# A decoder layer with a recurrent state and 64 routed experts: other loads at the start, states ordered head first, routing one iteration later

## The reference

```python
x = L0_attn_x
xn = _layernorm(x, axis=-1)
x = x + _L0_attn_ref(xn, ...) + _L0_ffn_ref(xn, ...)
```

```python
def step(Sst, inp):
    q_t, k_t, v_t, b_t, g_t = inp
    Sst = Sst * g_t[..., None, None]
    kS = jnp.einsum('bhk,bhkv->bhv', k_t, Sst)
    Sst = Sst + b_t[..., None, None] * jnp.einsum('bhk,bhv->bhkv', k_t, v_t - kS)
    o_t = jnp.einsum('bhk,bhkv->bhv', q_t, Sst)
    return (Sst, o_t)
```

## Time and profile before

| | us |
|---|---|
| median of 3 runs | 2108.34 |
| lowest, highest | 2107.29, 2110.54 |
| the profiled execution | 2116.39 |
| its span, first to last instruction | 2114.7 |
| mean granted TensorE clock, share of full speed | 0.808 |

### The profile page before, as it was taken

One profiled execution on the slowest core, in us unless ns is written; L12 is line 12 of the kernel. 1 busy time (PEld: TensorE's weight loads), 2 busy tenths in 40 slices (PEclk: granted clock), 3 DMA queues, 4 the chain that ended last, 5 costly groups with the idle time before them and its releaser, 6 DMA issues. The chain is left out here.

```text
span 2114.7 us, 32382 instructions
## 1 busy us (share of the span) xinstructions
PE 1507.1 (71%) x8894; PEld 1306.1 (62%) x8894; DVE 1863.5 (88%) x6189; ACT 876.7 (41%) x2296; POOL 1629.1 (77%) x1340
## 2 busy tenths in 40 slices
PE   6477878887751777655656558887888888868538
PEld 5467767776641666555555547776777777757336
DVE  3149999999998899999998798999999999999990
ACT  3355465546530442323423246545554344333113
POOL 4527888788886778877878689888888889888861
PEclk9778878877875877778777669988999899979677
DMA  8634233433336545565454621233222311111111
GB/s 192 154 90 119 60 86 88 131 89 85 87 82 155 140 115 134 138 177 138 104 143 125 169 64 53 61 99 93 64 57 73 106 51 43 54 54 35 38 35 26
DMA packets 302281, 201.30 MB, mean 95 GB/s; under 512 B 176210, under 2 KB 289556, under 8 KB 302100
## 3 DMA queue, kind: packets, MB, share of 16 engines
q1 hardware_dynamic: 283780, 165.40, 28.8%
q0 software_dynamic: 16208, 33.56, 7.2%
q10 hardware_dynamic: 2112, 0.26, 0.1%
HBM read 127.58 MB, written 71.60 MB: 94 GB/s over the span
## 5 line engine op out<-in xcount | busy, mean ns | idle before, releaser
L795 POOL TENSOR_TENSOR rp<-S,qs 128x2048 f32<-128x2048 f32 x113 | 514.0, 4549 | 173.8 <-DVE S L1087 128.9
L1087 DVE SCALAR_TENSOR_TENSOR S<-S,gwin,bank 128x256 f32<-128x256 f32 x1024 | 481.8, 471 | 1.1
L1081 DVE TENSOR_TENSOR bank<-nu,bank 128x256 f32<-128x256 f32 x1024 | 431.6, 421 | 1.1
L1071 DVE TENSOR_REDUCE bank<-prod 128x16 f32<-128x256 f32 x1024 | 429.9, 420 | 1.1
L1066 DVE TENSOR_TENSOR prod<-S,bank 128x256 f32<-128x256 f32 x1024 | 423.7, 414 | 0.5 <-DVE bank L1163 0.3
L1659 PE MATMUL bank<-region 128*128 128x128 f32 x2048 | 286.5, 300 | 0.0
L1659 PEld LDWEIGHTS bank<-region 128*128 128x128 f32 x2048 | 272.8, 214 | 16.3 <-issue 15.9
L803 POOL TENSOR_TENSOR r<-rp 128x1024 f32<-128x1024 f32 x113 | 274.8, 2432 | 7.1
L1670 PE MATMUL bank<-region 128*128 128x256 f32 x1024 | 236.7, 385 | 5.5 <-DVE region L1054 5.5
L1558 PE MATMUL bank<-xaT,wqkvg 128*128 128x128 f32 (+1 forms) x1792 | 236.1, 290 | 3.3 <-ACT xaT L1267 3.0
L1076 DVE SCALAR_TENSOR_TENSOR nu<-bank,gwin,win_v 128x16 f32<-128x16 f32 x1024 | 234.3, 229 | 1.1
(11 more groups left out here) (155 smaller groups left out, 2479.1 us busy)
## 6 DMA issues: line engine op xcount, KB each, us to landing
qkv_d<-stg SPq DMA_DIRECT2D x64, 384.0 KB, 4.1
region<-in_L_ffn_w_gate SPq DMA_DIRECT2D x64, 192.0 KB, 3.4
region<-in_L_ffn_w_up SPq DMA_DIRECT2D x64, 192.0 KB, 3.8
region<-in_L_ffn_w_down SPq DMA_DIRECT2D x64, 192.0 KB, 4.3
win_k<-qkv_d SPq DMA_DIRECT2D x16, 512.0 KB
win_q<-qkv_d SPq DMA_DIRECT2D x16, 512.0 KB
win_v<-qkv_d SPq DMA_DIRECT2D x16, 512.0 KB
region<-in_L_attn_x SPq DMA_DIRECT2D x32, 256.0 KB, 4.4
```

The source lines that it names most:

```text
L795: g.tensor_tensor(rp[:, :, :].rearrange("p (a v) d -> p a v d", v=DH), S[h][:, lo:lo + HS].rearrange("p t s (v d) -> p (t s) v d", v=DH), ...
L1071: m[G] = mark(v.tensor_reduce(kS[:, G], prod[:, G].rearrange("p (v d) -> p v d", v=DH), AX.X, ALU.add))
L1081: m[G] = mark(v.tensor_tensor(outer.rearrange("p (v d) -> p v d", v=DH), nu[:, G].unsqueeze(2).to_broadcast([P, DH, DH]), key(s, G), ALU.m ...
L1087: ins = v.scalar_tensor_tensor(S[h][:, s, G], earlier(h, s, G), gwin[:, I // NB2 & 1, G, 1, t:t + 1], outer, ALU.mult, ALU.subtract)
```

## The change

- SyncE loads blocks 0 to 3 of x and the ln1 weights' matrices first, straight to where they are used; ScalarE's queue loads ln1's gain and bias, which are applied to the transposed tile at its evacuation (two instructions in place of one) and no more to the weights. Constants for routing and the back are loaded behind the 16 stores, and block 4 of x with them. Blocks 5 to 7 are loaded in iterations 2 to 4, and the statistics and factors of blocks 4 to 7 are taken in iterations 1 to 4.
- The factors are worked out from the variance in closed form: one power for the front, one for routing, a block at a time.
- Partitions of states are ordered (head, sequence) where they were (sequence, head); the o stores are two DMAs where they were one.
- Block 0's window is loaded by GpSimd's queue, keys first; a separate semaphore tells of keys. VectorE squares and sums the keys of half 1 and scales block 0's keys.
- Routing iterations are 1 to 16, all later stages one iteration later; iteration 0 has a front tile only. The back's iteration without a tile is gone.
- The queries' copy stands at the end of every iteration. The window's load stands before the iteration's front store.

Cut to its core:

```diff
-R1 = 2 * NB2
+NRT = 2 * NB2
+R0 = 1
+R1 = R0 + NRT
...
-REFILL = {SEG[1]: FILL + 23, SEG[2]: FILL + 27}
+REFILL = {SEG[1]: FILL + 23, SEG[2]: FILL + 26}
...
-    counts = (3, 2, 3, 2, 3, 2, 3, 2, 2, 2, 3, 3, 0, 1, 2, 1)
+    counts = (3, 2, 3, 2, 3, 2, 3, 2, 2, 2, 3, 3, 1, 2, 1)
...
+LATE = 3
 FST = 2 * 16
-WLD = 5 * 16
+WLD = 4 * 16
+KLD = 16
+OST = 2 * 16
...
-        qkv_ld = qkv_d.rearrange("k (s b) (m g) (h d) t -> k m s b (g h) (d t)", s=2, m=3, h=P // DH)
-        gat_ld = gat_d.rearrange("k (s b) w h t -> k s w b h t", s=2)
-        o_st = o_d.rearrange("k (s b) g (h v) t -> k (b g h) s (v t)", s=2, h=P // DH)
+        qkv_ld = qkv_d.rearrange("k (s b) (m g) (h d) t -> k m s (g h) b (d t)", s=2, m=3, h=P // DH)
+        gat_ld = gat_d.rearrange("k (s b) w h t -> k s w h b t", s=2)
+        o_st = o_d.rearrange("k (s b) g (h v) t -> k s (g h) b (v t)", s=2, h=P // DH)
...
+            key_in, rest_in = keys_in(k, s)[0], window_in(k, s)[0]
+            queue.dma_start(win[1][:, par, s].rearrange("p d t -> p (d t)"), qkv_ld[k, 1, s]).then_inc(key_in, 16)
+            queue.dma_start(win[2][:, par, s].rearrange("p d t -> p (d t)"), qkv_ld[k, 2, s]).then_inc(rest_in, 16)
+            for w in range(2):
+                queue.dma_start(gwin[:, par, s, w], gat_ld[k, s, w]).then_inc(rest_in, 16)
+            queue.dma_start(win[0][:, par, s].rearrange("p d t -> p (d t)"), qkv_ld[k, 0, s]).then_inc(rest_in, 16)
...
-
             for m, w in enumerate((Wq, Wk, Wv)):
-                sp.dma_start(wraw[:, :, m * D:(m + 1) * D], w.rearrange("(c p) n -> p c n", p=P)).then_inc(raw_ld, 16)
+                sp.dma_start(wqkvg[:, :, m * D:(m + 1) * D], w.rearrange("(c p) n -> p c n", p=P)).then_inc(raw_ld, 16)
             for m, w in enumerate((Wb, Wg)):
-                sp.dma_start(wraw[:, :, 3 * D + m * H:3 * D + (m + 1) * H],
+                sp.dma_start(wqkvg[:, :, 3 * D + m * H:3 * D + (m + 1) * H],
                              w.rearrange("(c p) n -> p c n", p=P)).then_inc(raw_ld, 16)
-            for m, w in enumerate((ln1_g, ln1_b, ln2_g, ln2_b)):
-                sp.dma_start(lncol[:, m, :], w.rearrange("(c p) -> p c", p=P), allow_slow_non_contiguous=True).then_inc(raw_ld, 16)
+            for k in range(1, 4):
+                load_xs(sp, k)
...
+                done = f_stored[i] if k else first_st[q // (NB2 // 2)][i]
+                sp.dma_start(qkv_st[k, q], stg[i].rearrange("p b i t -> p (b i) t")).then_inc(done, 16)
+                sp.dma_start(gat_st[k, q], gst[i].rearrange("p (b t) -> p b t", b=2)).then_inc(done, 16)
...
-                window_half(k + 1, (k + 1) & 1, (k + 2) * NB2, s)
+                for i in range(BUF):
+                    sp.wait_ge(f_stored[i], (min((k + 1) * NB2 + s, NT - NB2) + 1 - i) // 2 * FST)
+                sp.sem_inc(passed, 1)
+                window_loads(sp, k + 1, (k + 1) & 1, s)
...
+            for f in range(AHEAD * NB2):
+                front_store(f, f // NB2, f % NB2, f % 2)
+                if f == NB2 + 1:
+                    for i in range(2):
+                        sp.sem_inc(xt_ld[i], AHEAD * NB2 // 2 * 16)
+                        front_load(AHEAD * NB2 + i, AHEAD, i, i)
...
+            load_xs(sp, 4)
+            sp.dma_start(wo_s[:, :, :], Wo.rearrange("(c p) n -> p c n", p=P)).then_inc(mlp_in, 16)
+            sp.dma_start(bo_s[:, :], bo.rearrange("(a n) -> a n", a=1)).then_inc(mlp_in, 16)
+            sp.dma_start(b1_in[:, :], b1.rearrange("(c p) -> p c", p=P), allow_slow_non_contiguous=True).then_inc(mlp_in, 16)
+            for m, w in enumerate((ln2_g, ln2_b)):
+                sp.dma_start(lncol[:, 2 + m, :], w.rearrange("(c p) -> p c", p=P), allow_slow_non_contiguous=True).then_inc(mlp_in, 16)
...
+                if 2 <= I < 2 + LATE:
+                    sp.wait_ge(xs_used, I + 3)
+                    load_xs(sp, I + 3)
...
+                    if 0 <= i < NRT - 1:
+                        route_load(i + 1, (i + 1) // NB2, (i + 1) % NB2, (i + 1) % 2)
                     if j < 2:
                         next_window(I // NB2, j)
-                    if I > 1:
-                        weights_store(I - 2)
-                        count_store(I - 2)
+                    front_store(f, f // NB2, f % NB2, h)
...
+            def front_factors(k):
+
+                lo, hi = k * NB2, (k + 1) * NB2
+                pool.wait_ge(xs_used, k + 1)
+                link(g.tensor_scalar(tmp_st[:, lo:hi], var[:, lo:hi], 1.0 + EPS, EPS * EPS, ALU.mult, ALU.add))
+                g.tensor_scalar(nmean[:, lo:hi], mean[:, lo:hi], -1.0, None, ALU.mult)
+                link(power(sA[:, lo:hi], tmp_st[:, lo:hi], 0, hi - lo))
+                g.tensor_tensor(bA[:, lo:hi], nmean[:, lo:hi], sA[:, lo:hi], ALU.mult).then_inc(stats_done, 1)
+
+            def route_factors(k):
+
+                lo, hi = k * NB2, (k + 1) * NB2
+                pool.wait_ge(stats_done, k + 1)
...
+                link(power(rstd[:, lo:hi], tmp_st[:, lo:hi], 0, hi - lo))
+                g.tensor_tensor(nmr[:, lo:hi], nmean[:, lo:hi], rstd[:, lo:hi], ALU.mult).then_inc(rstd_done, 1)
+
+            for k in range(2):
+                front_factors(k)
+            for k in range(2):
+                route_factors(k)
+            for k in range(2, 4):
+                front_factors(k)
+                route_factors(k)
             relink()
+            for s in range(2):
+                for i in range(BUF):
+                    pool.wait_ge(first_st[s][i], NB2 // 4 * FST)
+                pool.sem_inc(passed, 1)
+                window_loads(pool, 0, 0, s)
...
+            scale_values(0, 0)
+            square_sums(0, 0)
+            scale_values(0, 1)
             scale_gates(0)
-            for s in range(2):
-                scale_keys(0, s)
+
...
+                    if 1 <= I <= 1 + LATE:
+                        front_factors(I + 3)
+                        route_factors(I + 3)
...
+                    for s in range(2):
+                        g.dma_start(o_st[I // NB2, s], oblk[:, s].rearrange("p v t -> p (v t)")).then_inc(o_stored, 16)
...
+            def late_stats(k, part, c):
+
+                if part == 0:
+                    dve.wait_ge(xs_ld[4], 32 * (k - 3))
+                    for q in range(NB2):
+                        c[0] = mark(v.bn_stats(bn6[:, q, :], xs[4][:, q, :]))
+                elif part == 1:
+                    dve.wait_ge(vch, c[0])
+                    for q in range(NB2):
+                        c[0] = mark(v.bn_aggr(mv8[:, q, :], bn6[:, q, :]))
+                else:
+                    dve.wait_ge(vch, c[0])
+                    link(v.tensor_copy(mean[:, k * NB2:(k + 1) * NB2], mv8[:, :, 0]))
+                    v.tensor_copy(var[:, k * NB2:(k + 1) * NB2], mv8[:, :, 1]).then_inc(xs_used, 1)
...
+            def first_squares():
+
+                dve.wait_ge(*keys_in(0, 1))
+                dve.wait_ge(n2_ready, 1)
+                link(v.tensor_tensor(sq[:, :], win[1][:, 0, 1].rearrange("p d t -> p (d t)"),
+                                     win[1][:, 0, 1].rearrange("p d t -> p (d t)"), ALU.mult))
+                dve.sem_inc(sq_ready, 1)
+                v.tensor_reduce(n2[:, 1, :], sq[:, :].rearrange("p (d t) -> p t d", t=BLK), AX.X, ALU.add).then_inc(n2_ready, 1)
+
+            def first_keys():
+
+                dve.wait_ge(rk_ready, 1)
+                for s in range(2):
+                    kw = win[1][:, 0, s]
+                    v.tensor_tensor(kw, kw, rk[:, s, :].unsqueeze(1).to_broadcast([P, DH, BLK]), ALU.mult).then_inc(keys_ready, 1)
+
+            first_squares()
...
+                    if r is not None and (R0 <= I < R1 or X0 <= I < X1):
+                        product((I - R0 if I < R1 else I - X0 + NRT) * RT + r, r)
+                    if 1 <= I <= 1 + LATE and s >= 5:
+                        late_stats(I + 3, s - 5, t_)
...
-            act.wait_ge(raw_ld, 16 * 9)
-            for c in range(DC):
-                a_.activation(wqkvg[:, c, :], wraw[:, c, :], ACT.Copy, scale=lncol[:, 0, c:c + 1]).then_inc(w_scaled, 1)
-            act.wait_ge(bias_mm, 1)
-            a_.activation(bqkv[:, 0:2], LG[:, 0:2], ACT.Copy, scale=DH ** -0.5).then_inc(bias_done, 1)
-            a_.activation(bqkv[:, 2:6], LG[:, 2:6], ACT.Copy).then_inc(bias_done, 1)
-            a_.activation(bqkv[0:2 * H, 6:7], LG[0:2 * H, 6:7], ACT.Copy).then_inc(bias_done, 1)
-            act.wait_ge(bias_done, 3)
+            for m, w in enumerate((ln1_g, ln1_b)):
+                a_.dma_start(lncol[:, m, :], w.rearrange("(c p) -> p c", p=P), allow_slow_non_contiguous=True).then_inc(ln_ld, 16)
...
-                a_.activation(xaT[i].rearrange("p c t -> p (c t)"), banks[0][:, 0:DC * P], ACT.Copy).then_inc(xaT_ready, 1)
+                for c in range(DC):
+                    last = a_.activation(xaT[i][:, c, :], banks[0][:, c * P:(c + 1) * P], ACT.Identity,
+                                         scale=lncol[:, 0, c:c + 1], bias=lncol[:, 1, c:c + 1])
```

(10 more changed lines are left out.)

271 lines of the change are left out of this document (114 added, 157 removed).

## The result

The changed kernel takes **2060.86 us** (2060.51 to 2063.19, four runs) where the kernel before took 2109.44 beside it (2107.29 to 2114.70): a ratio of 0.976, 95% interval 0.9736 to 0.9784. A second set of five runs gave 2060.65 and 0.9766 (0.9743 to 0.9788). The forecast was 2064, within 2048 to 2086. In the medians the change is worth 48.6 us.

A forecast was written before the change was run, and what follows sets the result against it. VectorE, busy 88% of the span, was taken as the bound. Terms -39 - 13.4 - 2 + 14.6 - 8 + 2 + 0.5 gave -45.3, rounded to -44: from median 2108.34 to 2064 us, range 2048 to 2086.

The forecast's parts named there:

- The start: Before the recurrence: VectorE's first key copies come at 72.5 instead of 111.72, 39 us earlier (range 66 to 84).
- The first routed product: Early recurrence: product at 113.3, VectorE there at 106.9; wait 6.4 in place of 19.8, 13.4 us less.
- The smaller waits behind it: Routed iterations after the first product: 2 us less, as late statistics fill time before the fourth product in iterations 1 to 4.
- Late statistics: Iterations 1 to 4: statistics of blocks 4 to 7 move in from the idle prologue, 14.6 us more VectorE work.
- The slower rival: Iterations 1 to 4: VectorE waits for blocks 4 to 7 of x to land; four waits, 59 us, 2123; 4%.
- The queries' copy: At each iteration's end it leaves the chain to the fourth product: 8 us fewer waits (0 to 16).
- The partitions' order: States' partitions and window loads: reordering changes no arithmetic count and later loads are covered; put at nothing.
- The tail: End of the kernel: o stores become two DMAs, only the last on the path, +0.5 us (0 to 1).
- The rival of slow stores: Start: window half 0 streaming beside the stores keeps them slow; start at 84 to 92, time about 2079; 20%.
- the extra evacuation instruction: Front tiles on ScalarE: 0.25 us a tile on the fourth product's chain, costing 2 us (0 to 4).
- the closed empty iteration of the back: Back tiles: closing their one empty iteration gives zero, from -4 to +6, TensorE late if too dense.
- The sum: Whole kernel: all terms give -45.3 us, rounded to -44, for a median of 2064.

The follow-up runs named there:

- experiment 6: Changed kernel with block 0's window loaded from SyncE's queue instead of GpSimd's: 2055.3 us, ratio 0.9746.
- experiment 4: Changed kernel with statistics and factors of all eight blocks taken ahead of the recurrence again: 2088.25 us, ratio 0.9876.
- route_at_0: Changed kernel with routing in iterations 0 to 15 again and later stages one earlier: 2101.13 us, ratio 0.9943.
- no_late_bn: Changed kernel without the statistics operations of blocks 4 to 7, factors copied from block 3's results: 2056.9 us, ratio 0.9736.

## Why the prediction was right, step by step

- **The start**, forecast at 72.5, came at 73.36 and 72.56. Inside the sum two errors cancelled. The last store landed later than I said (half 1 was asked for at 57.60, where I had it at 56.6, the wait for `gat_d` before tile 7 being 4.1 where I allowed 3 for stores held by the window), and the five loads took GpSimd 2.6 us where I had 3.5. The rest are the 0.9 us by which 73.36 is late. The reduction, which I priced at 1.2 from a row of the same size, took 1.87; it reads its input in strides where that row did not, which I take for the cause and did not test. I took the key scalings at 2.4 and they took 2.62; the lower bound was the right one as long as GpSimd leaves VectorE alone (2.25 each when it does not, experiment 6).
- **The first routed product**, forecast at 113.3 with a wait of 6.4, came at 114.95 with 7.06. Its chain is the one I laid out: front's last output at 89.1 (88.9), normalisation at 107.67 (106). I counted SyncE's ten loads at 0.7 each, 7 us together. They took 12.3 us from 90.50 to 102.80: there were thirteen, and two of them, the scattered ones, took 5.1 us.
- **The smaller waits behind it**, forecast at 2 us (and some 6 more by the copy), are the term that I undersized most. Up to iteration 18 VectorE's idle time falls by 28.6 us; the first product gives 12.7 of it, the other waits 15.9. Before, VectorE's waits for ScalarE's products outside the first one were 17.7 us; now they are 5.3. The reason that I gave, late statistics that fill the time in which the fourth product is late, does not carry: with the statistics left out these waits are 4.4. The shift is not the reason either, since they are 3.8 with routing from iteration 0. The copy's place is worth some 3 of the 12.4 (they are 8.2 and 7.9 with the copy in the middle). What released the other 9 stays open. VectorE's waits of the kernel after from 73 to 607:

```profile
DVE hg_s L1055 <- ACT sgu L1397: 12.4, 8, 7.1
```

- **Late statistics** were priced at their full 14.6 us. As work of VectorE that is right: without them it works 14.1 us less up to iteration 18 (experiment 4). Leaving out 13.4 us of them gave 8.5 up to iteration 18 and 4 to 6 in the time, in a run where waits and a held copy took a part back. So the price in time lies between 4 and 14 and is not known better. The slower rival, that they wait for their loads, did not happen: no wait for x stands in front of them.
- **The queries' copy** was forecast at -8, between 0 and -16. It is **+6 to +7** (+10 to +11 by the ratios), outside its own range. The step that failed is "at the iteration's end it is off that chain". True in the routed iterations, where it is worth 3. In the experts the waits went from one engine to another: VectorE had won 6.3 us by the first back product and lost them there to GpSimd's scatters. I had bounded the gain from both sides but excluded a loss without a reason.
- **The partitions' order** was put at nothing. It is worth 10 us at the start and 7 in all. The argument, that it changes no count of arithmetic and that later window loads are covered, left out the one load that is not covered, block 0's. I had priced no landing time for half 1 at all. With the heads first it hid behind the 8 us that GpSimd takes from asking for half 1 to the end of half 0's sums; with the sequences first it does not. That the start came out right here was luck.
- **The tail** was +0.5 and is 1.0 (58.7 against 57.7).
- **The rival of slow stores** (20%) did not come: one wait of 4.1 us instead of four. Between 38 and 75 a store landed 4.8 us after its issue (median), between the 3.2 and the 6.6 of the earlier trace rows.
- **Not tested**: the extra evacuation instruction (+2), the closed empty iteration of the back (0), the closed form of the factors and the direct loads at the start have no run of their own.
- **The sum** came out right partly by luck. In the traces the start is 38.4 us earlier (forecast 39), VectorE's idle time from the first key copies to the tail falls by 28.5 (forecast -13.4 - 2 - 8 + 2, that is 21.4), its work rises by 12.6 (14.6), and the tail by 1.0 (0.5). So the waits fall by 7 us more than forecast, although the copy cost 6 to 7 of them where it was to give 8: some 22 us more than I counted were released elsewhere, much of it without a known cause. The two terms that made up most of the sum, start and first product, were each right to 1 us.

## What to carry to other kernels

When the start of a bound engine is pulled forward, look for the next thing that it meets (here the first routed product), because an arrival there that does not move along turns what was won into a wait: key copies 7.8 us earlier, with a product 4.0 us earlier, gave 3.4, bringing the product's loads forward gave 7.6. A queue such as SyncE's is a serial list of prices, and what is needed first has to stand first, ahead of loads that nobody wants for a thousand microseconds. An operation taken off one chain has to be looked up on its reader's chain in every phase of the kernel: here the same move helped among the routed iterations and, by the traces, cost among the experts. And where stages are cut at one engine's steps, work and waits have to be told apart, because a shift moves work over the cuts.

## What the runs showed of the hardware

- A window load's landing time follows the order of its outermost dimension: 5.3 us with 16 heads outermost, 11.1 with 8 sequences, for the same 512 KB (medians of two), with the engines' busy share at 1.00 in both.
- VectorE's products with two inputs in SBUF and GpSimd's block one another: 2.62 and 2.35 us alone, 4.52 and 3.30 together. The Trainium skill, "SBUF — State Buffer", section "Who interferes with whom", calls the ports that the two share an exclusive lock that whoever starts first holds for the whole instruction. The trace agrees: in turns, VectorE's first (1.3), then GpSimd's (2.35), then VectorE's second (1.3) from 67.67 on would end VectorE's at about 72.6, and they end at 72.2.
- A small copy of VectorE's was held for the whole of a long product of GpSimd's: 4.51 us instead of 0.17 beside one of 4.52 (`route_at_0`), 2.27 beside one of 2.34 (`no_late_bn`).
- The loads that scatter single elements (L534) took SyncE 2.9 and 2.2 us to issue, where the other single ones of that stretch took 0.3 to 1.3.
- Two profiles of the same kernel differ stage by stage, not only in sum: 459.5 and 457.7 us from iteration 18 to 32, 73.36 and 72.56 at the start, spans of 2061.4 and 2058.0. One profile can't settle a term of 2 us.
